# A 524,288-edge graph attention kernel: the edge sort goes on with half of each row, the rest is handled apart

## The reference, cut to what matters

```python
src = concat([edge_index[0], loops]);  dst = concat([edge_index[1], loops])   # M = 16384 nodes
e = leaky_relu(a_src[src] + a_dst[dst], negative_slope=0.2)
ee = exp(e - segment_max(e, dst)[dst])
alpha = ee / (segment_sum(ee, dst)[dst] + 1e-16)
agg = segment_sum(h[src] * alpha[:, :, None], dst, num_segments=M)
scores = layernorm(agg).reshape(M, HEADS, NUM_EXPERTS).mean(1)   # top 2 of 4 experts gate the result
```

## Time and profile before

| | us |
|---|---|
| median of 3 runs | 3851.6 (3848.0 to 3858.2) |
| the profiled execution, its own time | 3831.2 |
| its span | 3829.6 |
| front, to the barrier | 1322.1 |
| `find_blocks` and `edge_tables` | 1322.1 to 1435.0 |
| `layers` | 1435.0 to 3829.6 |

### The profile page before, as it was taken

One profiled execution on the slowest core, in us unless ns is written; L12 is line 12 of the kernel. 1 busy time (PEld: TensorE's weight loads), 2 busy tenths in 40 slices (PEclk: granted clock), 3 DMA queues, 4 the chain that ended last, 5 costly groups with the idle time before them and its releaser, 6 DMA issues.

```text
span 3829.6 us, 50716 instructions
## 1 busy us (share of the span) xinstructions
PE 2611.3 (68%) x16023; PEld 1941.3 (51%) x16024; DVE 2878.4 (75%) x7979; ACT 1816.2 (47%) x3236; POOL 1133.4 (30%) x1200
## 2 busy tenths in 40 slices
PE   2888888888888720015667677676776767676689
PEld 1666666666666510013445455455554545455566
DVE  7999898988898652347777778777777787687774
ACT  1666666666666401112444445344444544444444
POOL 0000000000000014555545555455545555455400
PEclk7999999999999965556878788787878878788889
DMA  2111111111110123222222223223222222322200
GB/s 86 36 48 39 45 39 45 36 36 45 37 47 28 65 23 85 47 60 55 57 73 64 72 61 75 61 59 75 58 72 65 61 71 64 71 61 57 73 12 9
DMA packets 241379, 208.18 MB, mean 54 GB/s; under 512 B 86460, under 2 KB 174168, under 8 KB 240600
## 3 DMA queue, kind: packets, MB, share of 16 engines
q1 hardware_dynamic: 186984, 188.72, 16.9%
q0 software_dynamic: 37152, 14.34, 3.8%
q10 hardware_dynamic: 16976, 1.89, 0.6%
HBM read 158.15 MB, written 46.67 MB: 53 GB/s over the span
## 4 chain that ended last, share of the span: by engine, by line
POOL 23%; DMA 19%; issue 16%; PE 3%; DVE 2%; ACT 0%; POOLq 0%; DVEq 0%
POOL lay_got L1514 23%; DMA lay_got<-node_table,lay_idx 19%; PE lay_b_y L1563 1%; PE lay_b_z L1554 1%; DVE keep_x L1904 0%; DVE lay_xn L1939 0%; DVE lay_stats L1928 0%; POOLq L1512 0%; PE lay_b_b L1593 0%; ACT lay_att L1742 0%; PE lay_b_g L1627 0%; ACT L1686 0%; ACT lay_hid L1686 0%; PE lay_b_g L1643 0%; PE lay_b_g L1635 0%
## 5 line engine op out<-in xcount | busy, mean ns | idle before, releaser
L1514 POOL DMA_INDIRECT lay_got<-node_table,lay_idx x1152 | 1114.3, 967 | 1061.8 <-DMA lay_got<-node_table,lay_idx 827.4
L1563 PEld LDWEIGHTS lay_b_y<-lay_w,lay_hid 128*128 128x128 f32 x4096 | 547.0, 209 | 242.8 <-issue 198.3
L1686 ACT ACTIVATE lay_hid<-lay_b_z,lay_b 128x512 f32<-128x512 f32 x512 | 335.6, 682 | 597.4 <-PE lay_b_z L1554 580.7
L1563 PE MATMUL lay_b_y<-lay_w,lay_hid 128*128 128x128 f32 x4096 | 548.2, 291 | 77.7 <-DVE keep_x L1904 61.6
L1554 PE MATMUL lay_b_z<-lay_xin,lay_w 128*128 128x512 f32 x1024 | 591.6, 707 | 2.0 <-ACT lay_hid L1686 2.0
L191 DVE TENSOR_TENSOR sort_keys<-sort_keys 128x1024 f32<-128x1024 f32 (+1 forms) x272 | 399.0, 1467 | 11.3 <-DVE front_rms L109 0.5
L1540 PE MATMUL lay_b_att<-lay_parts,lay_oh 128*128 128x60 bf16 x1152 | 69.1, 215 | 494.5 <-DVE lay_parts L970 491.5
L192 DVE TENSOR_TENSOR sort_keys<-sort_keys 128x1024 f32<-128x1024 f32 (+1 forms) x272 | 397.4, 1461 | 0.0
L801 POOL MEMSET find_no_src<- 128x9 int32 x1 | 0.1, 108 | 1322.1 <-POOLq L46 1322.1
L1764 ACT ACTIVATE lay_unused<-lay_hub_wide,lay_halves 128x1152 bf16<-128x1152 uint16 x256 | 319.9, 1250 | 140.9 <-DMA lay_hub_wide<-sorted_dst 136.6
L961 DVE TENSOR_REDUCE lay_look<-lay_b_att 128x36 f32<-128x108 f32 x128 | 34.1, 267 | 446.3 <-DMA lay_got<-node_table,lay_idx 445.8
(11 more groups left out here) (344 smaller groups left out, 4832.2 us busy)
## 6 DMA issues: line engine op xcount, KB each, us to landing
lay_wide<-sorted_dst SPq DMA_DIRECT2D x128, 288.0 KB
lay_hub_wide<-sorted_dst SPq DMA_DIRECT2D x128, 288.0 KB
made<-front_y SPq DMA_DIRECT2D x128, 256.0 KB, 2.0
lay_y<-made SPq DMA_DIRECT2D x32, 1024.0 KB, 7.5
lay_got<-node_table,lay_idx POOLq DMA_INDIRECT x1152
front_adj<-in_adj SPq DMA_DIRECT2D x32, 256.0 KB, 3.1
keep_x<-in_x SPq DMA_DIRECT2D x32, 256.0 KB, 3.4
lay_adj<-in_adj SPq DMA_DIRECT2D x32, 256.0 KB
```

The costliest lines, as they stand in the source:

```text
L1514: pool.indirect_dma_start(out=got[:, b % RING, c, :], out_offset=None, in_=table, in_offset=bass.IndirectOffsetOnAxis(ap=idx[:, b % AHEAD, ...
L1563: mm = pe.matmul(b_y[n % 2][:, P * j:P * j + P], hid[n % 2][:, c, P * j:P * j + P], w2[:, e * HK + c, :], start=(c == 0), stop=(c == HK - 1))
L1686: act.activation(hid[n % 2][:, c, :], b_z[c][:, :], ACT.Gelu, bias=b1[:, e * HK + c:e * HK + c + 1]).then_inc(hid_ready, 1)
```

## The change

The network sorts each row of 4096 keys by itself, as before, through level 11. At level 12 one stage of minimum and maximum splits every row into its lower and its upper 2048 keys. Only the lower ones go on (`net.cols` is 2048): their remaining stages are 2048 or 1024 columns wide, and a turned half has 8 pieces of 128x128 instead of 16 (`net.quarters` is 2 instead of 4). The number of halves that are turned stays 28. The upper keys are split further by `set_aside`, so that their lowest 128 of a row (the spill) stand apart.

What is left over is handled so. Hub edges in the spill are counted by one-hot products: in `layers`, 16 times 2 comparisons on DVE (`rest_hots_of`) and 128 matmuls on PE (`count_rest`). Any other valid edge that was left over is added in a loop over columns in `edge_tables`, which gathers the rows, adds and scatters the sum into `rest_sums` in HBM. The loop runs once when there is none, and 2048 times when there is one. For it, `att_far` is stored to HBM too (`rest_far`), `find_blocks` stores zeros and `rest_keys`, and `scores` loads and adds `rest_sums`, 16 times.

```diff
+        pos = self.run(pos, 0, 2 * cols, [cols], first=True)
+        self.rest = 1 - pos
+        for kind, n in (("rest", 2 * cols), ("sign", cols // 2)):
+            self.stages.append(Stage(self.total, pos, 0, n, 0, False, False, 0, False, kind))
...
-                    for q in range(4):
+                    for q in range(net.quarters):
...
+    hub_key, drop_key = (struct.unpack("f", struct.pack("I", (OFFSET + k * CLASS) << LOW_BITS))[0] for k in (1, 2))
...
+            sp.dma_start(rest_keys, bufs[net.rest][:, cols:2 * cols]).then_inc(stored, 16)
...
+            me.link(v.tensor_scalar(any_rest[:, :], banks[0][:, 2:3], 1.0, float(cols), ALU.min, ALU.mult))
+            me.mark(v.tensor_scalar(tables["rest"][:, :], any_rest[:, :], 1.0, None, ALU.max))
...
+            act.dma_start(rest_far[0:nodes, :].rearrange("(t n) f -> n t f", n=P), far[:, :, :]).then_inc(far_out, 16)
             act.wait_ge(table_out, 16)
             act.dma_start(hub_row[:, :], table[nodes - 1:nodes, :].broadcast_to([P, TAB])).then_inc(hub_in, 16)
...
+            v.sem_inc(rest_step, 1)
+            n = rest_count_of(v)
+            with v.Fori(0, n) as g:
+                v.wait_ge(rest_in, 16 * g + 16)
...
+            def load_rest(q):
+                after(sp, score_ready, q)
+                sp.dma_start(rest_sum[:, :, :], rest_sums[q * QT * P:(q + 1) * QT * P, :]
+                             .rearrange("(t n) f -> n t f", n=P)).then_inc(rest_in, 16)
...
+            def rest_hots_of(n):
+                S = [P, RC, P]
+                after(v, rest_used, n - 1)
+                for u, no in enumerate((keep["hub_node"], keep["hub_block"])):
+                    ins = v.tensor_tensor(rest_hots[n % 2][:, u, :, :], over(iota_b[:, :].unsqueeze(1), S),
+                                          over(no[:, RC * n:RC * n + RC].unsqueeze(2), S), ALU.is_equal)
```

More of the change, by code:

```diff
@@ L2 @@
 from contextlib import ExitStack
+import struct
 import concourse.bass as bass
@@ L109, in rsqrt @@
         me.link(v.scalar_tensor_tensor(out=y, in0=work, scalar=1.5, in1=y, op0=ALU.add, op1=ALU.mult))
-Stage = namedtuple("Stage", "start pos lo n d first directed turn half")
+Stage = namedtuple("Stage", "start pos lo n d first directed turn half kind")
 class Network:
@@ L140, in __init__ @@
-        for k in levels:
-            t = len(self.holds)
-            self.holds.append(pos)
[L144 to L148, removed]
+            pos = self.run(pos, 0, 2 * cols, [1 << j for j in reversed(range(k))], first=True, directed=True)
@@ L161, in run, with ends, set_aside @@
         return pos
[L163 to L166, removed]
+    def ends(self, pos, distances, turned, first=False, directed=False):
+        half = self.cols // 2
+        last = len(distances) - 1
+        for i, d in enumerate(distances):
+            if 0 < i < last or not (self.holds or i):
+                pos = self.run(pos, 0, self.cols, [d])
+                continue
+            for h in range(2):
+                after = self.run(pos, h * half, half, [d], first=first and i == 0, directed=directed and i == 0,
+                                 turn=0 if i else self.quarters * (turned + h + 1), half=i == last)
+            pos = after
+        return pos
+def set_aside(v, me, bufs, scratch, net, pos):
+    here, at = bufs[pos][:, net.cols:], 0
+    n = net.cols // 2
+    while n >= P:
+        low = bufs[1 - pos][:, net.cols:net.cols + P] if n == P else scratch[:, at:at + n]
+        me.mark(v.tensor_tensor(low, here[:, 0:n], here[:, n:2 * n], ALU.min))
+        me.mark(v.tensor_tensor(bufs[1 - pos][:, net.cols + n:net.cols + 2 * n], here[:, 0:n], here[:, n:2 * n], ALU.max))
+        me.wait()
+        here, at, n = low, at + n, n // 2
 def exchange(v, me, bufs, stage):
@@ L976, in add_sum, with edge_tables @@
     return v.tensor_tensor(here, here, added[:, :], ALU.add)
-def edge_tables(nc, w, sorted_src, sorted_dst, tables, table, keep):
+def edge_tables(nc, w, sorted_src, sorted_dst, rest_keys, rest_sums, rest_far, tables, table, keep):
     tiles = keep["x"].shape[1]
@@ L1241, in rank, with layers @@
     me.link(v.tensor_reduce(out, beat, AX.X, ALU.add))
-def layers(nc, adj, sorted_src, sorted_dst, first, table, made, w, keep, out):
+def layers(nc, adj, sorted_src, sorted_dst, rest_sums, first, table, made, w, keep, out):
     x, acc, far_parts = keep["x"], keep["acc"], keep["far"]
```

293 lines of the change are left out of this document (235 added, 58 removed).

## The result

The changed kernel takes 3834.65 us (median of 7 runs, 3827.85 to 3849.84) against 3851.6 us before (7 runs, 3844.7 to 3858.19): a ratio of 0.9959, with a 95% interval of 0.994 to 0.9979, so 17 us faster. The total came within 4 us of the forecast. One step inside it did not: `edge_tables` grew by twice what was forecast.

The account below looks back on a forecast made before the run. It took PE and ACT to set the front's period and POOL's gathers to pace `layers`. Terms -37 (turning), -5 (group 0), -12 (`find_blocks`), +31 (`edge_tables`), +2 (`layers`) give -21 us: 3851.6 to about 3831 us, range 3798 to 3862.

Parts of the forecast that it names:

- The bound of the front: Front: PE and ACT set the quiet period, 36.2 us; about 300 us less DVE work would show nearly nothing.
- The rival of a front bound by DVE: Front: DVE sets the pace after all and its 300 us come out, about 3565 us; chance 0.03.
- The turning: Front, groups from 12 on: halves turned by PE and ACT cost 45 us instead of 81.9, a gain of 37 us.
- waits in the same slot: Front: 4 us added where a turned pair in slot 4 or 0 is needed by a stage in the same slot.
- The rival that turning saves little: Front: pairs in slot 4 make DVE late for the norms; gain 10 instead of 37 us, 3858 us; chance 0.18.
- `find_blocks`: Stage where DVE is alone on the path: halved passes and counts minus additions, net 12 us less, between 9 and 14.
- `edge_tables`: Set-up stage, a chain of DMAs: `rest_far` store plus one round of the new loop, +31 us, between 16 and 48.
- The far store: `edge_tables`: storing `rest_far` in 16384 pieces of 16 B adds 13 us, bounds 2 and 16, ahead of the hub row's load.
- The round: `edge_tables`: one pass of the new left-over loop takes 18 us, lower bound 14, upper bound 32.
- the set-up costs more than all the rest gives: `edge_tables`: loop holes and slow landings add 48 us; with a turning gain of 20, 3861 us; chance 0.08.
- `layers`: Comparisons covered by POOL's gathers (38 us if not), `rest_sums` loads nearly free: +2 us, between 0 and 13.
- Rival 3: The rival about the set-up in `edge_tables` costing more than the rest gives: +48 us there, 3861 us; chance 0.08.

Follow-up runs that it names:

- e_dve: Changed kernel plus one no-effect DVE pass over 4096 columns (4.4 us) in every front group, between `rms` and the sort; 3831.6 us against 3833.3 before.
- e_defer: Changed kernel with the DVE stages of groups 18 and 25 that need a half turned in the same slot 4 put off to the next group's slot 0; 3810.1 us.
- a_again: The changed kernel, unchanged, run and traced a second time; 3820.0 us, ratio 0.9946 to the kernel before.
- after: The first profiled execution of the changed kernel, unedited; span 3848.1 us, the longest of its seven runs, whose median is 3834.65 us.
- e_piece32: Changed kernel with each node's four values in the `rest_far` store padded to 32 bytes, in SBUF and HBM; 3808.8 us against 3831.2 before.
- e_nohots: Changed kernel without the counting of spilled hub edges in `layers` (comparisons, matmuls, addition of counts); 3819.3 us, ratio 0.9952 to the kernel before.
- e_norest: Changed kernel without the `rest_far` store and the left-over loop, still loading and adding `rest_sums`; 3768.0 us, ratio 0.9823 to the kernel before.
- the second pair: The second traces of both unchanged kernels, b_again (before) and a_again (changed); 3840.2 and 3820.0 us.
- b_again: The kernel before the change, unchanged, run for a second trace; 3840.2 us (one run).
- e_far_t: Changed kernel storing `rest_far` in SBUF order, 128 pieces of 2 KB, with the row number computed in the loop; 3794.1 us, ratio 0.9892 to before.
- e_spread: Changed kernel with each partition's dropped key scattering to its own spare row of `rest_sums`; 3802.9 us, ratio 0.9908 to the kernel before.
- e_best: Changed kernel with the edits of e_far_t, e_spread and e_defer together; 3767.8 us, ratio 0.9826 to the kernel before.

## Why the prediction was right, and where not

**The bound of the front: right.** It said that PE and ACT set the period, and that 300 us less sort work on DVE would only lengthen DVE's wait. In the front DVE is 284 us less busy, the quiet period did not move by 0.1 us, and e_dve shows the same from the other side. Of the forecast 6 to 9 us more of waiting in every group, L734 and L725 show 5.9. The rival of a front bound by DVE is dead.

**The turning: right in size, and in mechanism as far as shown.** 45 us beyond the quiet period were forecast, and counted from group 1 it is 41.3: a gain of 40.7 us instead of 37. The part of it for waits in the same slot was too small (4 against about 7 by e_defer), and the turning itself cost less than put down (34 against 41). Group 1 came 4.1 us earlier (121.76 against 125.87), and 4.8 in a_again, instead of 5. The rival that turning saves little fails with that; its mechanism exists, but with 7 us and not with 27. No run changed the transposes alone. That the gain is theirs and not DVE's rests on e_dve, which gives DVE half of its saved work back for 1.5 us.

**`find_blocks`: right**, 13.8 and 13.9 us against 12, or 13 counted from POOL's first instruction.

**`edge_tables`: wrong.** The step was "+31 us, between 16 and 48", and it measured 66.4 and 56.7, outside its bounds. The prediction had itself named a store that lands in 30 us as a sign of being wrong. Without the part behind the node table the store took 31.1 us in after, so by that trace the sign came, and 26.4 in a_again. Two terms of the step were too small:

- The far store: "I take 13 us, with 2 and 16 as bounds". DVE's wait for the hub row grew by 29.8 and 24.5 us. The pieces were priced at the rate of the nearest row, 96 bytes each, and that rate holds down to 32 bytes (11.6 us in e_piece32) but not at 16. The upper bound had no row for such a short piece, so nothing in the trace supported it.
- The round: "18 us", of which "a scatter 0.95 and its landing 3.1". It measured 35.9 and 33.3 us. With distinct rows it is 14.5 us, near the lower bound of 14. The scatter's landing was taken from a gather, and the rows that it writes were left out of account. The count of the data was already there: the real edges past the lower half are all hub edges, so the loop sees only dropped keys, and these all go to one row.

The rival "the set-up costs more than all the rest gives" named the right place and the wrong mechanism. It blamed holes when engines leave a loop. There is one of 7.3 us before the second instruction of `layers` on POOL (L1686), as there was in the earlier trace rows, and none in the loop. It did not decide, since the front gave its gain in full.

The Trainium skill, "DMA: Bandwidth & Descriptors", section "Specifications", says that below 512 bytes a transfer does not reach the line rate, because the DMA engine then reads, changes and writes back. By that alone all of these pieces, 16 to 96 bytes, would be in one class. The runs show a further step below it: 26.9 us to land for 32 and 64 bytes, 40.5 to 46.4 for 16.

The formula that the prediction quotes from the Trainium skill, "DMA: Bandwidth & Descriptors", section "Anatomy of one DMA", is there a fit for DMAs that GpSimd issues. This store is issued from ACT, so the case is no test of the formula; nothing in the sum hangs on it.

**`layers`: as forecast for the work added.** The comparisons are covered (e_nohots), and the loads of `rest_sums` cost nothing that can be seen (e_norest).

**Slips in its sums.** Rival 3 comes to 3865 us by the prediction's own terms (-20 - 5 - 12 + 48 + 2), not 3861, and so lies just above the range's end at 3862. All good bounds together are -58 us with the 9 us for group 0, not -54. Neither changes the forecast.

**Why the total was still close.** By stages, the second pair gives -52.7 - 13.9 + 56.7 - 9.8 = -19.7 us, and with the pieces between and behind them (+1.4) the spans' -18.3. The miss of 26 us in `edge_tables` was made up by 12 us more in front and `find_blocks` in that pair, of which 6.6 are b_again's own longer front, and by a gathers' stretch 12 us shorter than the +2 forecast. That second part is not settled. Over the eleven profiled kernels with the loop the stretch is 2157.2 to 2185.7 us with a mean of 2168.8, and without it 2175.0, 2178.0 (before) and 2175.3 (e_norest). By the ratios, e_far_t loses 26 us against e_norest where its `edge_tables` grows by 34, e_spread 33 for 37, e_nohots 50 for 60 and a_again 47 for 58. All four lose less than the stage grows, by 4 to 11 us, but e_norest's interval alone is 10 us to either side. So it is not shown that anything gives time back in the gathers' stretch. POOL's waits for gathers vary from 793.0 (e_spread) to 823.6 us (after) between these kernels, and no run changed only that. So the near hit of the total is partly luck: a miss of 26 us against two of 12 us with the other sign.

## What to carry to other kernels

Before pricing a cheaper instruction, look who waits for whom at the end of the period: an engine at 75% busy gave nearly nothing for 284 us of its work, while the gain of 41 us came with 32 us less of transposes on a neighbour at 68%. Price a DMA by the number of its pieces only with a row of that piece size, store in SBUF's order where the reader can compute the address, and look what stands behind a slow store in its queue. For a scatter, ask which rows it writes in the case that really happens: an idle lane needs a spare row of its own.

## What the runs showed of the hardware

- 16384 stores of 16 bytes behind the node table took 40.5 to 46.4 us to land, of 32 bytes 26.9, of 64 bytes 26.9. A pitch of 64 bytes between the 16-byte pieces left it at 45.2. As 128 pieces of 2 KB the same data had landed 15.5 us after its issue, 0.6 us behind the node table ahead of it.
- An indirect scatter of 128 rows of 80 bytes took 20.4 to 22.8 us when all went to one row, and 2.2 us when each had its own (e_spread, e_best). The Trainium skill, "DMA: Bandwidth & Descriptors", section "Rules for kernel authors", asks for distinct target rows within a DMA since only one of the writes to a row remains. The time that a repeated row cost here was 18 to 21 us. Gathers of 16 bytes from one row by all 128 partitions took 3.1 us and from distinct rows 2.4.
- The issue itself was held up while many pieces were outstanding. On ACT's queue the far store took 12.84 us to issue, in after and in e_far_t, right behind the node table's store. The hub row's load of 12 KB took 21.0 to 28.2 us to issue behind the 16-byte pieces, 9.0 and 9.6 behind those of 32 and 64 bytes, and 0.33 in e_far_t.
